# Counts stage of a graph network: rings of four for ScalarE's source lanes and columns, copies of sums three steps behind, one turning moved by a step

## The chip, the cores and the metric

The kernel runs on one core of a Trainium2 chip. The metric is the device time of one execution in microseconds (us). A core has five engines that work side by side and wait for each other through semaphores: PE (TensorE, matrix products), DVE (VectorE), ACT (ScalarE), POOL (GpSimd) and SP (SyncE, which here issues transfers). Each has a queue of its own that also runs its loops, register moves and branches. PSUM holds PE's results, SBUF everything else that is on the core.

## The reference

A graph of 3125 nodes with 96 features and 103125 directed edges goes through four layers, each with a residual sum and a layer norm:

```
edge_index = stack([src, dst])                                   # edges sorted by dst
x = layernorm(x + L0(x))   # 10 steps of h = segment_sum(h[src] * dinv[src] * dinv[dst], dst)
x = layernorm(x + L1(x))   # attention over the edges, 4 heads
x = layernorm(x + L2(x))   # message by edge type (8), 2 layers
x = layernorm(x + L3(x))   # 2 layers of two linear maps, summed over the edges
```

All layers use the same edges. So the kernel first turns the list of edges into a dense matrix of counts (how many edges go from node to node) and one of codes (which types they have), and the layers then multiply by it. The change is in the stage that makes these two matrices.

## The kernel before, in words

The nodes are padded to 3200 = 25 tiles of 128 (NT = 25). A tile of destinations has 8 windows of 16 (WPT = 8, DW = 16), 200 windows in all; a window has two halves of 8. The edges of a half window lie in some chunks of 128 edges (one in each partition); a group holds 3 chunks of each half (GRP = 3, PAIR = 6). With these inputs each window needs one group, so the inner loops over `groups` run once. For each window:

- POOL, `records`: reads from the table `tile_tab` in SBUF where the chunks of each half begin (two register loads, made by `load`, L358), waits until ACT has read the slot of the ring `rec` (RECS = 4 slots) that it will write, and copies the records of the chunks there with two small copies (L445).
- ACT, `chosen`: copies the source lane and the value of each record into `sel` (L627) and works out the column of each edge in the window into `col` (L629, with the window's offset `woff` as bias). Both have two slots, and L627 waits until DVE has made the codes of the window two before.
- DVE: makes one-hot matrices by comparing with `iota`: `srchot` (128 lanes of source, from `sel`, L474), `hot` (200 columns for each half, from `col`, L477), and `codehot` = `srchot` times the value (L480). Two slots each; L474 waits until PE has used those of two windows before.
- PE, `window`: opens a PSUM bank of `codes` and one of `counts` with two products of zeros (L550; RING = 3 banks each, so it waits first for ACT's copy of the window three before), multiplies `srchot` by `hot` for the six chunks (L555), then `codehot` by `hot` (L560), and closes with a product of zeros (L564).
- ACT, `window_out`: copies the window's counts into `ct`, the matrix in SBUF (L604), and its codes into `stage` (L606). This is done two windows behind: in the slot of window w, after `chosen`, come the sums of w - 2.
- PE, `turn_round`, and ACT, `row_out`: the tile before this one is transposed in four rounds of up to seven blocks (L572), each followed by a copy to `crow` that also sums up the degrees (L614). `turned_after` says after which of PE's windows a round comes; ACT takes the same round two windows later.
- SP: stores `stage` by quarters of a tile, 200 KB each, when both windows of the quarter are copied (L668); the tile's row of `crow`, 800 KB, behind quarter 2 of the tile after it (L677); and the tile's `ct`, 800 KB, behind its own quarter 3 (L672). SP works through these strictly in order.

The order of the work on each engine is thus written out by hand, and only semaphores tie the engines together. In a ring, the wait for a free slot is on a count kept in registers: `past` holds how many groups were done when earlier windows began. In `records`, `free` is the register `past[0]` itself, read after the moves have shifted it.

In the last tile ACT also takes the first of three square roots, in the slot of window 2 (`root(0)`, L649). After the last window DVE scales the features and splits them in two halves for the first layer (L496 to L503), and with that the stage ends. The first product of the next stage starts at 440.76 us.

Of the kernel before, what the change touches and what calls it, by code (L numbers as in the profile page):

```python
# [7 lines left out]
F16 = mybir.dt.float16  # L8
BF16 = mybir.dt.bfloat16
# [4 lines left out]
ACT = mybir.ActivationFunctionType  # L14
# [62 lines left out]
def gnn_kernel(nc, a, out):  # L77

    with ExitStack() as top:
# [283 lines left out]
        assert WC <= 256 and len(rounds) == NR and 2 * WC <= 512 and 2 * NR == WPT and WPS == 2 * WPT  # L363
        RING = 3

        turned_after = {1: 0, 3: 1, 4: 2, 5: 3}
        RECS = 4
        LAG = 5
        assert WPT % RECS == 0
        with ExitStack() as ph:  # L370
# [17 lines left out]
            s_sq, s_sqo = sem("l0_sqrt_in"), sem("l0_sqrt_out")  # L388
            rec = wqk[:, 114:114 + RECS * 2 * PAIR].rearrange("p (k g c) -> p k g c", k=RECS, c=2)
            rec_sv = wqk[:, 114:114 + RECS * 2 * PAIR].bitcast(F16).rearrange("p (k g c) -> p k g c", k=RECS, c=4)  # L390
            sel = wqk[:, 162:162 + 2 * PAIR].bitcast(F16).rearrange("p (k c g) -> p k c g", k=2, c=2)
            col = wqk[:, 174:174 + PAIR].bitcast(BF16).rearrange("p (k g) -> p k g", k=2)
            assert 114 + RECS * 2 * PAIR <= 162
            s_rec = sem("cnt_rec")
            assert NW * (NCHP // GRP) + 2 < 1 << 16
            s_col = sem("cnt_col")
# [23 lines left out]
            with nc.Block() as block:  # L420
# [34 lines left out]
                @block.vector  # L455
                def _(e):
                    c = Chain(e, s_prep)
                    e.memset(zero, 0.0).then_inc(s_zero, 1)
                    e.wait_ge(s_xt, 1)
                    e.tensor_reduce(xone[:], counts[0:1, 2, 0:P], AX_X, ALU.max).then_inc(s_xone, 1)  # L460
                    n, past, free = three(e, "dve")
                    every = lambda v, m: v.unsqueeze(1).to_broadcast([P, GRP, m, 2])
                    each = lambda v, m: v.rearrange("p (g c) -> p g c", c=2).unsqueeze(2).to_broadcast([P, GRP, m, 2])

                    def tile(t):
                        groups = groups_of(e, t)
                        for w in range(WPT):
                            k = w % 2
                            e.reg_mov(free, past)
                            e.reg_mov(past, n)  # L470
                            with e.Fori(0, groups):
                                e.wait_ge(s_used, e.snap(free) + 1)
                                e.wait_ge(s_sel, e.snap(n) + 1)
                                e.tensor_tensor(srchot[:, k, :, :, :], every(iota[:, 2, 0:P, :], P), each(sel[:, k, 0, :], P),  # L474
                                                ALU.is_equal).then_inc(s_one, 1)
                                e.wait_ge(s_col, e.snap(n) + 2)
                                e.tensor_tensor(hot[:, k, :, :, :], iota[:], each(col[:, k, :], WC),  # L477
                                                ALU.is_equal).then_inc(s_hot, 1)
                                e.wait_ge(s_one, e.snap(n) + 1)
                                e.tensor_tensor(codehot[:, k, :, :, :], srchot[:, k, :, :, :], each(sel[:, k, 1, :], P),  # L480
                                                ALU.mult).then_inc(s_code, 1)
                                e.reg_add(n, n, 1)
                                e.reg_mov(free, n)

                    def degrees(i):
                        ts = PARTS[i]
                        e.wait_ge(s_turn_out, NR * ts.stop + 2)
                        c(e.tensor_reduce(deg[:, ts], dacc[:, ts, :], AX_X, ALU.add))
                        c(e.tensor_scalar(dinv[:, ts], deg[:, ts], 1.0, None, ALU.max))
                        c(e.tensor_scalar(some[:, ts], deg[:, ts], 1.0, None, ALU.min))  # L490
                        e.reciprocal(rdeg[:, ts], dinv[:, ts]).then_inc(s_sq, 1)

                    def rows_scaled(i):
                        ts = PARTS[i]
                        e.wait_ge(s_sqo, i + 1)
                        c(e.tensor_tensor(dinv[:, ts], dinv[:, ts], some[:, ts], ALU.mult))  # L496
                        c(e.scalar_tensor_tensor(val[:, ts, :], x[:, ts, :], scale[:, 0:1],
                                                 dinv[:, ts].unsqueeze(2).to_broadcast([P, ts.stop - ts.start, D]), ALU.mult, ALU.mult))

                    def rows_split(i):  # L500
                        ts = PARTS[i]
                        c(e.tensor_copy(u[0][:, ts, 0, :], val[:, ts, :]))
                        c(e.tensor_tensor(u[0][:, ts, 1, :], val[:, ts, :], u[0][:, ts, 0, :], ALU.subtract))  # L503

                    with e.Fori(0, NT - 1) as t:
                        tile(t)
                    degrees(0)
                    tile(NT - 1)

                    power_of_two(c, e, power[:], xall[:], scale[:, 0:1])  # L510
                    c(e.tensor_scalar(scale[:, 1:2], power[:], 2.0 ** -14, None, ALU.mult))
                    rows_scaled(0)
                    e.wait_ge(s_used, e.snap(n) + 1)
                    rows_split(0)
                    degrees(1)
                    ROUND_UP = 12582912.0
                    c(e.tensor_scalar(gc[:, 1:2], gc[:, 1:2], ROUND_UP, -ROUND_UP, ALU.add, ALU.add))
                    c(e.tensor_tensor(gc[:, 1:2], gc[:, 1:2], gc[:, 0:1], ALU.subtract))
                    c(e.tensor_scalar(gc[:, 1:2], gc[:, 1:2], (GG - 1) / 2, 1.0 / GG, ALU.add, ALU.mult))
                    c(e.tensor_scalar(gc[:, 1:2], gc[:, 1:2], ROUND_UP, None, ALU.add))  # L520
                    last_tile = ident[0:NT, NT - 1:NT]
                    c(e.tensor_scalar(gc[:, 1:2], gc[:, 1:2], -ROUND_UP, last_tile, ALU.add, ALU.add))
                    c(e.tensor_scalar(gc[:, 1:2], gc[:, 1:2], float(SLOTS), last_tile, ALU.max, ALU.subtract))
                    c(e.tensor_copy(gi[:, 1:2], gc[:, 1:2]))
                    c(e.tensor_scalar(gc[:, 1:2], gc[:, 1:2], -float(GG), float(NCHG), ALU.mult, ALU.add))
                    c(e.tensor_scalar(gc[:, 0:1], gc[:, 0:1], gc[:, 1:2], None, ALU.min))
                    e.tensor_copy(gi[:, 0:1], gc[:, 0:1]).then_inc(s_gtab, 1)
                    rows_scaled(1)
                    rows_split(1)
                    degrees(2)  # L530
                    rows_scaled(2)
                    rows_split(2)
# [61 lines left out]
                def _(e):  # L594
# [20 lines left out]
                                     ACT.Copy, accum_out=dacc[:, bass.ds(t, 1), q]).then_inc(s_turn_out, 1)  # L615

                    e.sem_inc(s_code, 1)
                    n, past, free = three(e, "act")

                    def chosen(t, w, groups):  # L620

                        e.reg_mov(free, past)
                        e.reg_mov(past, n)
                        with e.Fori(0, groups):
                            e.wait_ge(s_rec, e.snap(n) + 1)
                            e.wait_ge(s_code, e.snap(free) + 1)
                            e.activation(sel[:, w % 2, :, :], rec_sv[:, w % RECS, :, 0:2].rearrange("p g c -> p c g"),  # L627
                                         ACT.Copy).then_inc(s_sel, 1)
                            e.activation(col[:, w % 2, :], rec[:, w % RECS, :, 1], ACT.Identity,  # L629
                                         bias=woff[:, bass.ds(t * WPT + w, 1)]).then_inc(s_col, 1)  # L630
                            e.reg_add(n, n, 1)
                            e.reg_mov(free, n)

                    def tile(t, first, second, last=False):
                        groups = groups_of(e, t)
                        for w in range(WPT):
                            chosen(t, w, groups)
                            if w >= 2:
                                window_out(t, w - 2, first)
                            elif not first:  # L640
                                window_out(t - 1, WPT - 2 + w, second)
                            if not first and w - 2 in turned_after:
                                row_out(t - 1, turned_after[w - 2], second)
                            if last and w == 2:
                                root(0)
# [7 lines left out]
                    with e.Fori(2, NT - 1) as t:  # L653
                        tile(t, False, False)
                    tile(NT - 1, False, False, True)
                    window_out(NT - 1, WPT - 2, False)
                    window_out(NT - 1, WPT - 1, False)
                    for q in range(NR):
                        row_out(NT - 1, q, False)
                        if q == 0:  # L660
# [1844 lines left out]
```

## Time and profile before

| | us |
|---|---|
| median of three runs | 2363.64 (2362.68 to 2366.68) |
| the profiled execution, its own time | 2366.91 |
| its span | 2365.2 |
| the counts stage in it, about | 47 to 440 |

Over the whole span the page has PE busy 91%, DVE 77%, ACT 49%, POOL 37%. These are means over stages with different limits. In the page's 40 slices of 59 us the counts stage is slices 1 to 7: there DVE is at 8 and 9 tenths, PE and ACT at 8, POOL at 4. The granted clock is at 9 tenths and more of the full 2.4 GHz in nearly all slices.

How to read the rows below: times are from the start of the span; a group of instructions is named by line, engine and operation, with what it writes and reads (`out<-in`). Several tensors are views of larger ones, and rows name those: `rec`, `sel` and `col` are parts of `wqk`, `srchot`, `crow` and `stage` parts of `flat`, `hot` and `codehot` parts of `onehots`. Idle time before an instruction is put down to what seems to have ended it. Register loads, moves and branches are in an engine's queue (POOLq, ACTq) and not in its busy time.

### The profile page before, as it was taken

Reading aid. Unit: us, or ns where it says so; the run is one execution under the profiler, and the core shown is the slowest. Engines: PE = TensorE matmul, PEld = TensorE weight load, DVE = VectorE, ACT = ScalarE, POOL = GpSimd, SP = SyncE. Lnnn points to the kernel's source line nnn. Section 1 sums busy time; section 2 is a strip of 40 time slices with the busy share of each in tenths; the row PEclk is TensorE's granted clock in tenths of the full one; section 3 lists DMA queues with packets and bytes.
Section 4 is the critical chain, followed back from the end, with each engine's and each line's share of the span. In section 5 each row is a group of like instructions: output and inputs, shape, how many; then the busy total and the mean of one; then the engine's idle time right before and its main releaser. Section 6 shows DMA issues by size and latency. Waiting matters only on the chain. (4 is left out here: it accounts for less than half of the span.)

```text
span 2365.2 us, 63175 instructions
## 1 busy us (share of the span) xinstructions
PE 2159.4 (91%) x22505; PEld 1795.4 (76%) x22506; DVE 1832.0 (77%) x2687; ACT 1162.6 (49%) x2789; POOL 879.4 (37%) x1062
## 2 busy tenths in 40 slices
PE   2888888799999999888999978999999999999897
PEld 2777777799999999622222225999996799999787
DVE  8899988765655566578999976988886788887446
ACT  1888888432332333388999966231322432230323
POOL 3444444000000000067888832555552455555000
PEclk8999999899999999989999979999998999999899
DMA  2344444200100000242222224223224322222800
GB/s 67 153 166 165 164 166 159 106 30 30 43 30 30 29 29 15 65 108 57 57 57 59 57 97 159 84 73 88 75 60 127 139 74 77 85 75 45 343 11 22
DMA packets 94785, 205.64 MB, mean 87 GB/s; under 512 B 21718, under 2 KB 61270, under 8 KB 94450
## 3 DMA queue, kind: packets, MB, share of 16 engines
q1 hardware_dynamic: 81458, 182.46, 22.3%
q0 software_dynamic: 13120, 20.18, 4.3%
q8 instruction: 159, 2.61, 0.5%
q14 instruction: 48, 0.39, 0.1%
HBM read 116.99 MB, written 84.76 MB: 85 GB/s over the span
## 5 line engine op out<-in xcount | busy, mean ns | idle before, releaser
L1873 PE MATMUL l_bank<-tab,mask 128*128 128x192 f16 x7600 | 636.3, 247 | 8.3 <-PEq L1704 3.5
L1873 PEld LDWEIGHTS l_bank<-tab,mask 128*128 128x128 f16 x7600 | 629.5, 98 | 10.8 <-issue 10.2
L1459 DVE TENSOR_SCALAR mask<-code 128x1600 int32<-128x1600 int32 x304 | 546.7, 1816 | 91.6 <-PE l_bank L1873 82.7
L1849 POOL DMA_INDIRECT ggot<-table_dram,gidx x408 | 386.2, 947 | 264.7 <-PE l_bank L1873 204.0
L1356 DVE TENSOR_TENSOR pr<-ex,count_copy 128x1568 f32<-128x1568 f32 x200 | 351.0, 1786 | 24.7 <-POOL ex L1255 12.8
L1346 ACT ACTIVATE ex<-score_pair,poss 128x784 f32<-128x784 f32 x400 | 344.0, 910 | 30.0 <-PE score_pair L1294 18.6
L1255 POOL TENSOR_SCALAR ex<-ex 128x1568 f32<-128x1568 f32 x200 | 298.5, 1493 | 78.2 <-ACT ex L1346 71.1
L891 PE MATMUL sums<-onehots,ct 128*128 128x192 f16 x3125 | 266.5, 250 | 11.6 <-issue 7.3
L891 PEld LDWEIGHTS sums<-onehots,ct 128*128 128x128 f16 x3125 | 263.9, 99 | 14.1 <-issue 7.9
L891 PE MATMUL sums<-u,ct 128*128 128x192 f16 x3125 | 259.1, 246 | 0.0
L891 PEld LDWEIGHTS sums<-u,ct 128*128 128x128 f16 x3125 | 258.0, 98 | 0.0
L445 POOL COPY wqk<-edges 128x6 f32 x400 | 162.4, 435 | 244.9 <-ACT wqk L629 133.2
L950 DVE TENSOR_REDUCE onehots<-sums 128x96 f32<-128x192 f32 x250 | 89.2, 357 | 178.7 <-PE sums L891 177.7
L1933 ACT ACTIVATE gidx<-rowidx 128x12 int32 x34 | 7.2, 211 | 426.2 <-PE l_bank L1881 396.1
L1294 PE MATMUL score_pair<-qa,ka 96*128 96x392 f16 x800 | 205.7, 340 | 3.6 <-ACT ex L1346 2.2
L1294 PEld LDWEIGHTS score_pair<-qa,ka 96*128 96x128 f16 x800 | 47.4, 98 | 184.9 <-ACT ex L1346 176.3
L1310 PE MATMUL att_acc<-pr,v 128*32 128x392 f32 x1600 | 176.6, 513 | 5.6 <-DVE pr L1356 5.6
L555 PE MATMUL counts<-onehots,flat 128*128 128x200 f16 x1200 | 145.9, 257 | 33.2 <-DVE onehots L477 31.2
L868 POOL PARTITION_ALL_REDUCE wtop<-wmax x1 | 0.4, 374 | 434.7 <-DVE wmax L981 434.7
L477 DVE TENSOR_TENSOR onehots<-iota,wqk 128x1200 f16<-128x1200 f16 x200 | 155.3, 776 | 0.0
L560 PE MATMUL codes<-onehots 128*128 128x200 f16 x1200 | 143.6, 255 | 0.0
L474 DVE TENSOR_TENSOR flat<-iota,wqk 128x768 f16<-128x768 f16 x200 | 111.7, 558 | 39.4 <-ACT wqk L627 32.6
(344 smaller groups left out, 2873.0 us busy)
## 6 DMA issues: line engine op xcount, KB each, us to landing
code<-code_dram SPq DMA_DIRECT2D x38, 800.0 KB
code_dram<-flat SPq DMA_DIRECT2D x100, 200.0 KB, 1.9
ct_dram<-ct SPq DMA_DIRECT2D x25, 800.0 KB, 3.5
c_dram<-flat SPq DMA_DIRECT2D x25, 800.0 KB, 3.4
ct_again<-ct_dram SPq DMA_DIRECT2D x25, 800.0 KB, 17.3
cring<-c_dram SPq DMA_DIRECT2D x200, 98.0 KB, 1.9
table_dram<-tab SPq DMA_DIRECT2D x50, 384.0 KB, 2.3
flat<-code_dram SPq DMA_DIRECT2D x19, 800.0 KB, 4.4
```

Source lines behind the costliest of these rows:

```text
L445: ins = e.tensor_copy(rec[:, w % RECS, h * GRP:(h + 1) * GRP, :], edge_rec[:, bass.ds(chunks[h], GRP), :])
L477: e.tensor_tensor(hot[:, k, :, :, :], iota[:], each(col[:, k, :], WC), ALU.is_equal).then_inc(s_hot, 1)
L555: e.matmul(counts[:, b, h * WC:(h + 1) * WC], chunk_of(srchot, k, j), chunk_of(hot, k, j), start=False, stop=False, skip_group_check=True)
L891: mm = e.matmul(sums[t % RS][:, 0:2 * D], ct[:, t, s, :], u[par][:, s, :, :].rearrange("p k d -> p (k d)"), start=(s == 0), stop=(s == NT ...
L1255: ins = e.tensor_scalar(ex[n % UR][:], ex[n % UR][:], EXP_HIGH, EXP_LOW, ALU.min, ALU.max)
L1294: mm = e.matmul(pair_ps[k][:, h, 0:QC], ka[0:D, k * HP2 + h, j * P:(j + 1) * P], qa[0:D, k * HP2 + h, b * QC:(b + 1) * QC], start=True, st ...
L1310: mm = e.matmul(acc[h * HW:(h + 1) * HW, b % 2, 0:QC], v[:, j, h, :], pr[n % UR][:, h, :], start=(j == 0), stop=(j == NT - 1), skip_group_ ...
L1346: e.activation(ex[n % UR][:, k * HP2:(k + 1) * HP2, :], pair_ps[k][:, :, 0:QC], ACT.Exp, scale=poss[:]).then_inc(s_ex[k], 1)
L1356: e.tensor_tensor(pr[n % UR][:], ex[n % UR][:], c_ps[n % 2][:, 0:QC].unsqueeze(1).to_broadcast([P, H, QC]), ALU.mult).then_inc(s_pr, 1)
L1459: e.tensor_scalar(turned.rearrange("p (s q d) -> p s q d", q=NQ, d=DQ // 2), words.rearrange("p (q s d) -> p s q d", q=NQ, d=DQ // 2), abs ...
L1849: e.indirect_dma_start(ggot[:, k, j, :], None, table_dram[:, :], bass.IndirectOffsetOnAxis(ap=gidx[:, k, j:j + 1], axis=0)).then_inc(s_ggo ...
L1873: mm = e.matmul(acc[k][:, 0:2 * D], mask[:, r % MR, s, :], tab[:, s, r, :], start=(r == 0 and s == 0), stop=(r == R - 1 and s == NT - 1))
```

## The change

`sel` and `col` get four slots (SELS) in place of two, and `col` moves from `wqk` to unused columns of `onehots`. DVE reads them by `w % SELS`. ACT keeps the same count of groups as POOL does, four windows back, so L627 of a window waits for the codes of the window four before. The sums are copied three windows behind (OUT_LAG = 3), so the last three windows of a tile are copied in the slots of windows 0, 1 and 2 of the next, and the last three of all after the loop. The first round of turning comes after window 2 of the next tile and not after window 1.

```diff
-        turned_after = {1: 0, 3: 1, 4: 2, 5: 3}
+        turned_after = {2: 0, 3: 1, 4: 2, 5: 3}
         RECS = 4
+        SELS = 4
+        OUT_LAG = 3
...
-            sel = wqk[:, 162:162 + 2 * PAIR].bitcast(F16).rearrange("p (k c g) -> p k c g", k=2, c=2)
-            col = wqk[:, 174:174 + PAIR].bitcast(BF16).rearrange("p (k g) -> p k g", k=2)
+            sel = wqk[:, 162:162 + SELS * PAIR].bitcast(F16).rearrange("p (k c g) -> p k c g", k=SELS, c=2)
+            col_at = 2 * PAIR * (P + WC) + 2 * NW
+            col = onehots[:, col_at:col_at + SELS * PAIR].bitcast(BF16).rearrange("p (k g) -> p k g", k=SELS)
...  DVE: sel[:, k, ...] and col[:, k, :] become sel[:, w % SELS, ...] and col[:, w % SELS, :]
-                    n, past, free = three(e, "act")
+                    n = e.alloc_register("cnt_act_done")
+                    past = [e.alloc_register(f"cnt_act_past{k}") for k in range(SELS)]
+                    for r in (n, *past):
+                        e.reg_mov(r, 0)
                     def chosen(t, w, groups):
-                        e.reg_mov(free, past)
-                        e.reg_mov(past, n)
+                        free = past[0]
+                        for k in range(SELS - 1):
+                            e.reg_mov(past[k], past[k + 1])
+                        e.reg_mov(past[SELS - 1], n)
                         with e.Fori(0, groups):
                             e.wait_ge(s_rec, e.snap(n) + 1)
                             e.wait_ge(s_code, e.snap(free) + 1)
...  ACT: sel[:, w % 2, ...] and col[:, w % 2, :] become sel[:, w % SELS, ...] and col[:, w % SELS, :]
                             chosen(t, w, groups)
-                            if w >= 2:
-                                window_out(t, w - 2, first)
+                            if w >= OUT_LAG:
+                                window_out(t, w - OUT_LAG, first)
                             elif not first:
-                                window_out(t - 1, WPT - 2 + w, second)
+                                window_out(t - 1, WPT - OUT_LAG + w, second)
...
-                    window_out(NT - 1, WPT - 2, False)
-                    window_out(NT - 1, WPT - 1, False)
+                    for w in range(WPT - OUT_LAG, WPT):
+                        window_out(NT - 1, w, False)
```

## Rows read from the trace of the kernel before

**Rows 1.** Windows view, 60 to 408 us: stretch, length, busy time of each engine, clock

```profile
60.00:408.00 348.00, 297.43 (x3357) 270.35 (x3355) 313.16 (x556) 293.14 (x923) 148.77 (x370) 0.99 0.41 161
```

**Rows 2.** Groups of DVE by line, 60 to 408 us: busy, mean | idle before

```profile
L474 DVE TENSOR_TENSOR flat<-iota,wqk 128x768 f16<-128x768 f16 x185 | 103.3, 558 | 34.8 <-ACT wqk L627 28.2 <-issue 4.0 <-PE codes L560 2.5
```

**Rows 3.** Timeline of POOL, tile 13: start, length, instruction, idle before

```profile
242.00 0.65 POOL L445 COPY wqk<-edges 128x6 f32 x2 [2.00 <-issue]
243.60 0.34 POOL L445 COPY wqk<-edges 128x6 f32 x2 [0.94 <-issue]
245.86 1.02 POOL L445 COPY wqk<-edges 128x6 f32 x2 [1.91 <-ACT wqk L629]
...
254.65 0.32 POOL L445 COPY wqk<-edges 128x6 f32 x2 [0.57 <-issue]
256.97 1.25 POOL L445 COPY wqk<-edges 128x6 f32 x2 [2.00 <-issue]
```

**Rows 4.** Timeline of POOL, last tile, its first and last pair

```profile
407.47 1.30 POOL L445 COPY wqk<-edges 128x6 f32 x2 [2.00 <-issue]
...
420.17 0.77 POOL L445 COPY wqk<-edges 128x6 f32 x2 [0.86 <-ACT wqk L629]
```

**Rows 5.** Timeline of ACT, tiles 12 and 13, and the last tile's table load

```profile
239.92 0.31 ACT L629 ACTIVATE wqk<-wqk,onehots 128x6 bf16<-128x6 f32 x1
...
247.00 0.21 ACT L627 ACTIVATE wqk<-wqk 128x12 f16<-128x12 f16 x1 [1.28 <-POOL wqk L445]
...
247.99 0.50 ACT L606 ACTIVATE flat<-codes 128x400 uint16<-128x400 f32 x1
...
254.69 0.22 ACT L627 ACTIVATE wqk<-wqk 128x12 f16<-128x12 f16 x1
...
256.64 0.25 ACT L627 ACTIVATE wqk<-wqk 128x12 f16<-128x12 f16 x1
...
415.07 1.28 ACT L649 ACT_TABLE_LOAD   x1
```

**Rows 6.** By line L358, three stretches: queue, ns min/median/max, first and last

```profile
L358 POOLq TENSOR_LOAD <-tile_tab x394: 273/278/889, 60.1 to 406.9; - x197
...
L358 POOLq TENSOR_LOAD <-tile_tab x2: 280/566/853, 244.3 to 244.7; - x2
...
L358 POOLq TENSOR_LOAD <-tile_tab x9: 273/275/312, 250.4 to 256.4; - x9
```

**Rows 7.** Timeline of SP, tile 13, issues; then DMA issues of the page: us to landing

```profile
243.78 0.33 SPq L677 DMA_DIRECT2D c_dram<-flat  x1
...
246.43 0.34 SPq L672 DMA_DIRECT2D ct_dram<-ct  x1
...
c_dram<-flat SPq DMA_DIRECT2D x25, 800.0 KB, 3.4
```

**Rows 8.** Timeline of DVE, tiles 13 and 24

```profile
243.95 0.56 DVE L474 TENSOR_TENSOR flat<-iota,wqk 128x768 f16<-128x768 f16 x1 [0.18 <-issue]
...
245.59 0.55 DVE L474 TENSOR_TENSOR flat<-iota,wqk 128x768 f16<-128x768 f16 x1
...
254.95 0.56 DVE L474 TENSOR_TENSOR flat<-iota,wqk 128x768 f16<-128x768 f16 x1 [0.45 <-ACT wqk L627]
...
414.16 0.56 DVE L474 TENSOR_TENSOR flat<-iota,wqk 128x768 f16<-128x768 f16 x1
...
416.73 0.56 DVE L474 TENSOR_TENSOR flat<-iota,wqk 128x768 f16<-128x768 f16 x1 [0.85 <-ACT wqk L627]
...
423.73 0.56 DVE L474 TENSOR_TENSOR flat<-iota,wqk 128x768 f16<-128x768 f16 x1
```

**Rows 9.** Timeline of PE, tile 24, windows 3 and 4

```profile
418.04 0.71 PE L555 MATMUL counts<-onehots,flat 128*128 128x200 f16 x6 [0.41 <-DVE onehots L477]
418.58 0.70 PE L560 MATMUL codes<-onehots 128*128 128x200 f16 x6
...
420.06 0.71 PE L555 MATMUL counts<-onehots,flat 128*128 128x200 f16 x6
```

More of the change, by code:

```diff
@@ L390, in gnn_kernel @@
             rec_sv = wqk[:, 114:114 + RECS * 2 * PAIR].bitcast(F16).rearrange("p (k g c) -> p k g c", k=RECS, c=4)
-            sel = wqk[:, 162:162 + 2 * PAIR].bitcast(F16).rearrange("p (k c g) -> p k c g", k=2, c=2)
-            col = wqk[:, 174:174 + PAIR].bitcast(BF16).rearrange("p (k g) -> p k g", k=2)
-            assert 114 + RECS * 2 * PAIR <= 162
+            sel = wqk[:, 162:162 + SELS * PAIR].bitcast(F16).rearrange("p (k c g) -> p k c g", k=SELS, c=2)
+            col_at = 2 * PAIR * (P + WC) + 2 * NW
+            col = onehots[:, col_at:col_at + SELS * PAIR].bitcast(BF16).rearrange("p (k g) -> p k g", k=SELS)
+            assert col_at + SELS * PAIR <= NT * 2 * D
+            assert 114 + RECS * 2 * PAIR <= 162 and 162 + SELS * PAIR <= 2 * D
             s_rec = sem("cnt_rec")
@@ L473, in tile @@
                                 e.wait_ge(s_sel, e.snap(n) + 1)
-                                e.tensor_tensor(srchot[:, k, :, :, :], every(iota[:, 2, 0:P, :], P), each(sel[:, k, 0, :], P),
+                                e.tensor_tensor(srchot[:, k, :, :, :], every(iota[:, 2, 0:P, :], P), each(sel[:, w % SELS, 0, :], P),
                                                 ALU.is_equal).then_inc(s_one, 1)
                                 e.wait_ge(s_col, e.snap(n) + 2)
-                                e.tensor_tensor(hot[:, k, :, :, :], iota[:], each(col[:, k, :], WC),
+                                e.tensor_tensor(hot[:, k, :, :, :], iota[:], each(col[:, w % SELS, :], WC),
                                                 ALU.is_equal).then_inc(s_hot, 1)
                                 e.wait_ge(s_one, e.snap(n) + 1)
-                                e.tensor_tensor(codehot[:, k, :, :, :], srchot[:, k, :, :, :], each(sel[:, k, 1, :], P),
+                                e.tensor_tensor(codehot[:, k, :, :, :], srchot[:, k, :, :, :], each(sel[:, w % SELS, 1, :], P),
                                                 ALU.mult).then_inc(s_code, 1)
@@ L626, in chosen @@
                             e.wait_ge(s_code, e.snap(free) + 1)
-                            e.activation(sel[:, w % 2, :, :], rec_sv[:, w % RECS, :, 0:2].rearrange("p g c -> p c g"),
+                            e.activation(sel[:, w % SELS, :, :], rec_sv[:, w % RECS, :, 0:2].rearrange("p g c -> p c g"),
                                          ACT.Copy).then_inc(s_sel, 1)
-                            e.activation(col[:, w % 2, :], rec[:, w % RECS, :, 1], ACT.Identity,
+                            e.activation(col[:, w % SELS, :], rec[:, w % RECS, :, 1], ACT.Identity,
                                          bias=woff[:, bass.ds(t * WPT + w, 1)]).then_inc(s_col, 1)
```

## The prediction

> **What bounds the kernel now.** The change touches one stage, some 47 to 440 us of the span, so I read that stage alone. First the busy times of its even part, 60 to 408 us: DVE is busy 313.16 of 348.00 us (90%), ACT 293.14, PE 297.43, POOL 148.77 (43%) [rows 1]. By busy time DVE bounds it, and its idle time lies before one instruction, L474: 34.8 us, of which 28.2 were ended by ACT's L627, the copy that fills `sel` [rows 2]. That is what a deeper ring would give back. So the question is who makes L627 late.
>
> Next, the order in time of POOL, which gathers the records that L627 copies. The pairs of copies (one pair for each window) start at 242.00, 243.60, 245.86 ... 254.65 and 256.97 [rows 3]. Windows 0 of tiles 13, 14 and 24 are the rows 242.00, 256.97 and 407.47 [rows 3, 4]: 14.97 us for one tile, 150.50 / 10 = 15.05 us for each of the next ten. That is the pace of the stage. The page puts POOL's idle time before 245.86 down to ACT L629. It can't be that one: the pair at 245.86 (tile 13, window 2) refills the slot of four windows earlier, whose L629 started at 239.92 and took 0.31 us [rows 5] (it is the fourth L629 before the one that follows L627 at 247.00, which copies this record). Its release was 5.6 us old. POOL waits for nobody here; it is slow by itself. What it does in the "idle" time stands under its queue: two register loads from `tile_tab` for each window (`records`, L439) and one for each tile, 394 in 60 to 408 us with a median of 278 ns [rows 6], and branches and register moves around them. The shortest step, 243.60 - 242.00 = 1.60 us, is that serial program with no disturbance; the step over a tile's end, with one load more, is 256.97 - 254.65 = 2.32. A tile undisturbed would be 7 x 1.60 + 2.32 = 13.5 us; 15.05 are observed, so 1.5 us a tile, some 36 us over 24 tiles, are disturbance.
>
> Third, what disturbs. A load of 853 ns lies in 243.3 to 246 us, and the nine of 249.6 to 257 take 273 to 312 ns [rows 6]. The two 800 KB stores of the tile are issued at 243.78 (L677) and 246.43 (L672) [rows 7]. So POOL's loads are slow while a big store runs, about 0.75 us for each store.
>
> The Trainium skill weighs against both readings. Its page "Perfetto Trace Analysis", section Identifying the Most-Contended Engine, takes the engine with the highest occupancy as the one to optimize; that would be DVE, and rival 1 is that case. The Trainium skill's "SBUF — State Buffer", section SBUF: two separate sides, says that DMA and engine accesses can't slow each other; for these register loads the trace disagrees (0.28 against 0.85 us beside a store), and by that rule the moved stores would be worth nothing.
>
> **The change part by part.** Sum against the profiled execution: 2366.91 us, span 2365.2; the runs have a median of 2363.64, 3.3 lower. I work out a difference and put it on the median.
>
> (a) `sel`/`col` rings of four (from two). ACT's L627 may then start when the codes of four windows ago are made, not two. ACT can't use this beyond one window: it needs the record, and L627 follows POOL's second copy at once wherever ACT is free. What ACT does gain is at most its own lateness: in tile 13 DVE waited 0.45 us before 254.95 [rows 8] while ACT was at a turned row. Where ACT is in time, the record isn't there: L627 at 247.00 starts 0.12 us after POOL's pair of 245.86 ends [rows 3, 5]. POOL's program has no wait that ACT would now end sooner, so the tile stays at 15.05 us. DVE's undisturbed step is 245.59 - 243.95 = 1.64 us [rows 8], 13.1 us a tile, still under POOL's pace. Saved in the even part: 0. Bounds: from below 0, from above the whole 28.2 us of rows 2.
>
> (b) Three register moves more per window on ACT. They run in ACT's queue while the activates before them are at work. 0; without that cover an estimated 0.1 us a window (a load that reads memory takes 0.28 [rows 6], moves must be far under it), which ACT's idle time takes: ACT is busy 84% [rows 1], 12.7 us of a tile's 15.05.
>
> (c) `OUT_LAG` 3: L604 and L606 copy a window's sums one slot later. PSUM has RING = 3 banks, and PE's window w waits for the copy of w - 3 (L548), which ACT now reaches only after `chosen` of w. L606 ends 247.99 + 0.50 - 247.00 = 1.49 us after L627 [rows 5], L474 starts 0.25 after L627, and PE's L555 starts 418.04 - 416.73 = 1.31 after L474 [rows 8, 9]: the copy is done 1.24 after L474. PE's two zeroing products stand between, so PE may start each window some 0.2 us later than now. That is a new wait on PE; queued behind it are the window's twelve products, and DVE waits for the last of them only two windows on: it ends 418.58 + 0.70 - 416.73 = 2.55 us after L474, two steps of DVE are 3.28, so 0.7 us are in hand. 0, bounds 0 and, were it all on the path, 0.2 x 200 = 40.
>
> (d) Turning of row 0 from after window 1 to after window 2, so windows 2, 3, 4, 5 all carry one on PE and slots 4, 5, 6, 7 on ACT (before: 1, 3, 4, 5 and 3, 5, 6, 7). A PE window with a turning takes 420.06 - 418.04 = 2.02 us [rows 9], four of them 8.1 (the last turns four blocks only), against 4 x 1.64 = 6.6 on DVE: PE falls 1.2 us behind in them. `hot` has two slots, so DVE of window 7 would wait for PE's window 5 by some 0.4 us, if DVE ran at its own pace. It doesn't, since two disturbed POOL steps fall there. Late in tile 24, it can. On ACT a slot with a row is 256.64 - 254.69 = 1.95 us [rows 5], four are 7.8 against POOL's 3 x 1.60 + 2.32 = 7.1: 0.7 us late at the next tile's window 0, made good in the slots that have no row.
>
> (e) Moved with (c) and (d): both stores, since SP waits for copies. L677 waits behind the quarter of windows 4 and 5, whose second copy moves a slot into the next tile, some 1.6 us later; L672 behind window 7, also 1.6 us. They stay as many and as large, and the time between them stays one to two slots. Each still meets POOL's pairs of loads: it lands 3.4 us after its issue [rows 7], of which I take the last 2 or so as moving data, and POOL comes round every 1.60. What a store costs depends on where the pair of loads falls: one load hit (0.57 us, from 0.85 - 0.28) at least, two (1.13) at most; before it was 0.75. Laying those 2 us over POOL's steps of tile 13, 1.6 us later than now, I estimate about 0.6 for L677 and 0.7 to 0.9 for L672, as before. 0, with bounds of (0.57 - 0.75) x 2 x 24 = -9 us and (1.13 - 0.75) x 2 x 24 = +18 us.
>
> (f) The end. In tile 24 ACT has the square root with its table load (1.28 us at 415.07 [rows 5]) after the copy of window 0's sums, in the new order after that of 23's window 7, whose sums are there sooner, so L474 of window 3 starts at 415.80 (414.16 + 1.64) and not at 416.73. Then DVE goes on at 1.64 up to window 5, and windows 6 and 7 wait for PE, which now turns in four windows in a row: window 7 at 423.1 and not 423.73 [rows 8]. POOL's last pair starts at 420.17 [rows 4] and isn't late. From there DVE's chain runs to the end of the stage, with no wait for another engine of over 0.3 us, and shifts with it: -0.6 us, bounds 0 and -2 (window 7 as soon as its record and DVE allow).
>
> Sum: 0 + 0 + 0 + 0 + 0 - 0.6: 2366.3 for the profiled execution, **2363.0 us** in the measure of the median.
>
> **Rivals.**
> 1. *DVE-bound.* If L627 is late by ACT's own fault, the rings give back the 28.2 us: 2335 us. For it: DVE's 90%. Against: POOL's starts sum to the tile's whole time with no release it waits for. 8%.
> 2. *Stores cheaper.* The stores land where a pair of loads is hit once: -9 us and the end's -1: 2354. For it: the phase is fixed by the kernel, the same in each tile, and will be another. 15%.
> 3. *Slower: stores dearer.* A store starts just as a pair of loads begins, both are hit, 24 times: up to +18, half of it if one of the two stores does so: 2372 to 2381. It decides once L677's data begin within 0.1 us before the first load of a pair. Nothing in POOL's program gives it back. 12%.
> 4. *Slower: four turnings in a row.* If ACT and PE late together hold up DVE by over 1.9 us a tile, the rest is lost each tile: 0.4 x 23 = +9: 2373. It needs ACT over 15.05 us a tile where it is busy 12.7, or PE's 0.2 of (c) to reach DVE. 4%.
>
> **How the numbers follow.** No change 61%, rival 1 8%, rival 2 15%, rival 3 12%, rival 4 4%. A measurement of this kernel tells 0.2%, 4.7 us, from no change. The likeliest's own range is 2359 to 2368. For 8 in 10 I take in most of rivals 2 and half of 3 and leave rival 1: 2353 to 2373. Faster 24%: rival 1, rival 2, and little of the main case's low side. Same 60%. Slower 16%: rivals 3 and 4.
>
> **What would show it.** Right: POOL's window 0 pairs still 15.05 us apart (14.7 to 15.4), its steps between stores 1.60, loads over 0.8 us only beside the stores; DVE's idle before L474 still over 25 us, now ended by L627 behind a POOL copy, less often behind L614. (c), (d): PE waits for ACT L606 or DVE for PE's L560 in windows 6 and 7. (e): issues of L677 and L672 1 to 2 us later against POOL. (f): L474 of the last window 0 to 2 us nearer to POOL's last pair. Wrong: POOL's steps under 1.60, or tiles under 14.5 us (POOL wasn't the pace), or over 15.6 (rival 3).

## The result, and the profile after

| | before | after |
|---|---|---|
| median of seven runs, us | 2363.64 (2361.87 to 2368.44) | 2372.59 (2368.60 to 2374.67) |
| the profiled execution | 2366.91 | 2374.67 |
| its span | 2365.2 | 2372.9 |

The ratio is 1.0032, with a 95% interval of 1.0021 to 1.0044: the changed kernel is slower by some 8 us. "No change" was forecast, at 2363.0 us; slower was given 16%.

The even part of the counts stage, in the view of rows 1, and DVE's group in the view of rows 2, both of the changed kernel:

```profile
60.00:408.00 348.00, 291.16 (x3261) 260.93 (x3259) 306.37 (x543) 288.00 (x898) 145.25 (x362) 0.95 0.41 157
```

```profile
L478 DVE TENSOR_TENSOR flat<-iota,wqk 128x768 f16<-128x768 f16 x181 | 101.0, 558 | 41.5 <-ACT wqk L636 23.7 <-PE codes L564 13.5 <-issue 4.0
```

Every engine does less in the same 348 us: four windows fewer (181 for 185). DVE's idle time rose from 34.8 to 41.5 us, and 13.5 of it are now ended by PE's codes, where it was 2.5. Read by itself that looks like the new waits of (c) and (d), and the waits view shows PE's too. Two rows of before, then the two that answer to them in the changed kernel, all for 60 to 408 us (who waits, for whom: us, times, longest):

```profile
PE codes L550 <- ACT flat L606: 14.6, 15, 1.2
...
DVE flat L474 <- PE codes L560: 2.5, 4, 0.9
```

```profile
PE codes L554 <- ACT flat L610: 51.4, 75, 2.3
...
DVE flat L478 <- PE codes L564: 13.5, 24, 1.5
```

But the stage's pace is still POOL's. Its timeline for tile 13 of the changed kernel, to be laid beside rows 3:

```profile
246.98 0.65 POOL L449 COPY wqk<-edges 128x6 f32 x2 [2.00 <-issue]
248.57 0.34 POOL L449 COPY wqk<-edges 128x6 f32 x2 [0.95 <-issue]
250.25 0.91 POOL L449 COPY wqk<-edges 128x6 f32 x2 [1.34 <-ACT onehots L638]
252.48 1.10 POOL L449 COPY wqk<-edges 128x6 f32 x2 [1.33 <-ACT onehots L638]
254.17 0.73 POOL L449 COPY wqk<-edges 128x6 f32 x2 [0.58 <-ACT onehots L638]
256.62 1.07 POOL L449 COPY wqk<-edges 128x6 f32 x2 [1.72 <-issue]
258.35 1.01 POOL L449 COPY wqk<-edges 128x6 f32 x2 [0.66 <-ACT onehots L638]
259.94 0.32 POOL L449 COPY wqk<-edges 128x6 f32 x2 [0.58 <-issue]
262.26 1.28 POOL L449 COPY wqk<-edges 128x6 f32 x2 [2.00 <-issue]
```

The tile takes 262.26 - 246.98 = 15.28 us, and the steps are 1.59, 1.68, 2.23, 1.69, 2.45, 1.73, 1.59, 2.32. The undisturbed 1.59 is still there. Two steps are long by 0.6 and 0.9 us, and three more by some 0.1. Of these three the first, the step behind window 1, is no disturbance: in every tile of both kernels it takes 1.67 us or more. SP's timeline of the same stretch (start, length, issue; L686 is the store of a turned row, L681 that of the tile's `ct`, L677 those by quarters) and POOL's register loads of the six steps from 248.57 on, each row one step (ns min/median/max):

```profile
250.38 0.33 SPq L686 DMA_DIRECT2D c_dram<-flat  x1
252.85 0.33 SPq L677 DMA_DIRECT2D code_dram<-flat  x1
253.39 0.34 SPq L681 DMA_DIRECT2D ct_dram<-ct  x1
256.59 5.14 SPq L677 DMA_DIRECT2D code_dram<-flat  x2
```

```profile
L358 POOLq TENSOR_LOAD <-tile_tab x2: 273/278/282, 249.2 to 249.6; - x2
...
L358 POOLq TENSOR_LOAD <-tile_tab x2: 311/597/883, 250.8 to 251.3; - x2
...
L358 POOLq TENSOR_LOAD <-tile_tab x2: 279/324/368, 253.1 to 253.5; - x2
...
L358 POOLq TENSOR_LOAD <-tile_tab x2: 547/708/869, 254.8 to 255.7; - x2
...
L358 POOLq TENSOR_LOAD <-tile_tab x2: 278/345/412, 257.2 to 257.7; - x2
...
L358 POOLq TENSOR_LOAD <-tile_tab x2: 273/277/281, 258.9 to 259.3; - x2
```

Loads of 0.88 and 0.87 us stand beside the two big stores, as before; the second pair is now hit twice (0.55 and 0.87). And two loads, 0.37 and 0.41 us, stand right behind the issues of *quarter* stores (252.85 and 256.59), which the prediction did not price.

The whole stage can be added up. POOL's queue between its first and its last pair holds register loads, other instructions and gaps. This table is worked out from all its records in each trace (us; "to DVE's last" is from POOL's last pair to the start of the last window's first one-hot, "rest" all that follows, "other" the other instructions of the queue and "gaps" the time between them; the copies run beside both and are not counted):

```
                  first pair  422 loads  other  gaps   first to last  to DVE's last  rest
before              47.76      152.3     123.3  96.8      372.40          3.56      1941.45
after               47.86      161.3     123.3  96.8      381.42          2.43      1941.22
```

Other instructions and gaps are the same to 0.1 us. A wait for another engine would be a longer gap, so the change makes POOL wait for nobody. Its loads take 9.0 us longer, the end gives back 1.1, and the start and the rest take -0.1: together 7.8, and the profiled executions are 2374.67 - 2366.91 = 7.76 us apart. The granted clock in the stretch fell from 0.99 to 0.95 of the full 2.4 GHz, with PE less busy; since POOL's time is accounted for by its loads, and "rest" is 0.2 us shorter, this is not where the time went.

### The profile page after: what moved, and what is told of

Its sections match the earlier page's. It is cut to its first block and busy times, and to the rows that moved or that the text cites. A ratio compares the mean times of both kernels' runs of the same rounds, so it can differ in the third digit from the quotient of the medians.

```text
span 2372.9 us, 63177 instructions
## 1 busy us (share of the span) xinstructions
PE 2161.2 (91%) x22505; PEld 1792.9 (76%) x22506; DVE 1829.7 (77%) x2687; ACT 1166.1 (49%) x2789; POOL 878.2 (37%) x1062
## 5 line engine op out<-in xcount | busy, mean ns | idle before, releaser
L1882 PEld LDWEIGHTS l_bank<-tab,mask 128*128 128x128 f16 x7600 | 629.4, 98 | 11.5 <-issue 10.7
L559 PE MATMUL counts<-onehots,flat 128*128 128x200 f16 x1200 | 151.4, 264 | 9.1 <-DVE onehots L481 3.8
L481 DVE TENSOR_TENSOR onehots<-iota,onehots 128x1200 f16<-128x1200 f16 x200 | 155.3, 776 | 0.0
```

The lines of the kernel that those rows point to most:

```text
L481: e.tensor_tensor(hot[:, k, :, :, :], iota[:], each(col[:, w % SELS, :], WC), ALU.is_equal).then_inc(s_hot, 1)
L559: e.matmul(counts[:, b, h * WC:(h + 1) * WC], chunk_of(srchot, k, j), chunk_of(hot, k, j), start=False, stop=False, skip_group_check=True)
L1882: mm = e.matmul(acc[k][:, 0:2 * D], mask[:, r % MR, s, :], tab[:, s, r, :], start=(r == 0 and s == 0), stop=(r == R - 1 and s == NT - 1))
```

## The experiments

All ratios are to the kernel before, run on the same chip beside it, with 95% intervals; 0.1% is 2.4 us. Its median was 2362.36 us beside the first group of runs (parts, one load), 2358.17 beside the second (deferred stores, packed table) and 2360.44 beside the third (parts on the packed table, quarters twice), so runs of different groups are compared by their ratios. GpSimd in the expectations is POOL.

**One part at a time.** Theory A: POOL's register loads, disturbed by stores whose phase against POOL moved. Theory D: the new waits of PE and DVE. (B: ACT's lateness is the pace. C: the rings' register moves cost. E, and later F: the four turnings in a row cost. G: the lag costs once POOL is off the path. In the expectation of `oneload_before` B stands for DVE and ACT as the pace, in that of `packed_before` for "POOL is not the pace".) The three parts were run alone.

```diff
# rings_only: the change, but
-        OUT_LAG = 3
+        OUT_LAG = 2
-        turned_after = {2: 0, 3: 1, 4: 2, 5: 3}
+        turned_after = {1: 0, 3: 1, 4: 2, 5: 3}
# lag_only: the kernel before, but
+        OUT_LAG = 3      # window_out(t, w - OUT_LAG), window_out(t - 1, WPT - OUT_LAG + w)
# turn_only: the kernel before, but
-        turned_after = {1: 0, 3: 1, 4: 2, 5: 3}
+        turned_after = {2: 0, 3: 1, 4: 2, 5: 3}
```

> Only the rings of four for sel and col; the sums are copied two steps behind and the first turning comes after window 1, as before. Theory A (GpSimd's serial program of register loads and copies paces the stage, and the change costs only by where the 800 KB stores meet its register loads): the stores stay where they were, so the time stays within 0.1% of the kernel before (2363.6 us) and GpSimd's 422 register loads between its first and last pair of copies still add up to about 152 us (161 in the changed kernel). Theory B (ACT's lateness is the pace, rings give it back): 20 to 28 us faster. Theory C (the rings themselves cost, by three more register moves on ACT): 3 to 9 us slower.

> Only the copies of the sums three steps behind (rings of two, first turning after window 1). Theory A: both 800 KB stores move by one to two steps and meet more of GpSimd's register loads, so most of the 9 us appear here: 2368 to 2373 us, loads 158 to 162 us in sum. Theory D (the cost is PE waiting for a PSUM bank that ACT now frees later, and DVE waiting for PE): also slower, but with the loads' sum at 152 us and idle time of DVE before L474 ended by PE's L560 over 8 us.

> Only the first turning moved from after window 1 to after window 2. Theory A: the stores are tied to the copies of the sums and not to this turning, and move by well under a step: within 0.15% of before, loads' sum 150 to 155 us. Theory E (four turnings in a row on PE and ACT are what costs): 4 to 9 us slower with the loads' sum at 152 us.

Measured: rings 2363.56 us, 1.0007 [0.9995, 1.0018]; lag 2371.73 us, 1.0043 [1.0027, 1.0059]; turning 2366.13 us, 1.0021 [1.0011, 1.0031], more than was expected of it. The rings can't be told from before, and the other two cost. The same sums over POOL's queue:

```
                  first pair  422 loads  other  gaps   first to last  to DVE's last  rest
rings_only          47.83      153.4     123.3  96.8      373.52          3.79      1937.52
turn_only           47.64      155.8     123.3  96.8      375.92          3.70      1934.95
lag_only            47.84      159.2     123.3  96.8      379.31          1.89      1938.46
```

Again only the loads differ: +1.1, +3.5 and +6.9 us, in the order of the times. For the lag Theory A's numbers held (2368 to 2373 us, loads 158 to 162). Of Theory D's two signs one is there, 22.7 us of DVE's idle time ended by PE, but the other, loads still at 152, is not, and POOL's gaps did not grow. With the ends (+0.2, +0.1, -1.7) this gives +1.3 us for the rings (1.0007 is 1.7), +3.6 for the turning (1.0021 is 5.0) and +5.2 for the lag, where 1.0043 is 10 with a low end of 6.4. The order holds, and the lag's size is not wholly found in its one profiled execution. The column "rest" shows why a single profile says so little of a few us: these stages are the same code and differ by up to 6.5 us. It is the loads of this stage, not a difference of two profiled totals, that carries the argument. The parts don't add up (1.1 + 6.9 + 3.5 = 11.5, together 9.0); a phase need not add up.

**Stores taken from the stage.** The stage's own 800 KB `ct` stores were moved to the next stage, in both kernels.

```diff
-                                if q == NQ - 1:
-                                    own(t - 1)
...  next stage, SP, behind each load of codes
+                            for j in range(2):
+                                own((kk - 1) * 2 * CPK + (2 * c + j))
```

> The kernel before, with the 800 KB store of each tile's counts (L672) taken out of the counts stage and issued in the next stage, two behind each code load. Theory A: about half of the 35.5 us that the stores cost GpSimd's register loads goes: a tile 14.3 us, loads' sum 133 to 140 us, 2343 to 2350 us. If something else paces the stage: no change.

> The changed kernel with the same store moved to the next stage. Theory A: it loses the own store's share of the 44.5 us, so 2346 to 2353 us, and is still 2 to 6 us slower than defer_before (the row's store and the quarters stay where the change puts them). Theory D (PE and ACT holding each other): 8 us or more slower than defer_before.

Measured: 2353.89 us, 0.9969 [0.9957, 0.9980], and 2356.14 us, 0.9988 [0.9977, 0.9999]. Both are slower than was expected of them (2343 to 2350 and 2346 to 2353). In the first the loads fell from 152.3 to 144.1 us, not to 133 to 140, and the last window of DVE starts 8.1 us earlier (415.65 against 423.73), against 7.3 by the ratio. The stores that remain hit more often than before (their share stands in the table of slow loads below). Of the changed kernel 145.6 us of loads are left, 1.5 more than of the one before: most of the 9.0 us went when this store went, though the phases of the others moved too. The 0.2% between the two is within the two intervals' reach.

**Loads taken from POOL.** If POOL's loads pace the stage, fewer must make it faster, and with POOL off the path Theory D's waits are seen alone. First, one load of two words instead of two loads of one; then both first chunks packed in one word of the table, one load, and two register operations.

```diff
# oneload_before
-                            for h in range(2):
-                                first = load(e, tile_tab[0:1, bass.ds(t, 1), 2 * w + h], 0, 2 * NCHP - GRP)
+                            _, firsts = nc.values_load_multi_w_load_instructions(
+                                tile_tab[0:1, bass.ds(t, 1), 2 * w:2 * w + 2]..., engines=[e.engine], ...)
+                            for first in firsts:
# packed_before, packed_after: table = second * 2048 + first, made once at the start
-                                first = load(e, tile_tab[0:1, bass.ds(t, 1), 2 * w + h], 0, 2 * NCHP - GRP)
+                            e.reg_load(both, tile_tab[0:1, bass.ds(t, 1), w:w + 1]...)
+                            e.reg_alu(firsts[0], both, 2047, ALU.bitwise_and)
+                            e.reg_alu(firsts[1], both, 11, ALU.logical_shift_right)
...
+                                first = e.snap(firsts[h])
```

> The kernel before, with GpSimd's two register loads of a window made one load of two registers (same values). Theory A: GpSimd's undisturbed step falls from 1.60 to 1.25 to 1.30 us, under DVE's 1.64, so GpSimd stops being the pace; a tile falls from 15.05 to 13.4 to 14.0 us and the kernel to 2325 to 2340 us; GpSimd begins to wait for ACT's L629. Theory B (DVE and ACT are the pace): no change within 0.2%.

> The kernel before, with the two first chunks of a window packed in one word of the table (first + 2048 * second, made by VectorE at setup), so GpSimd does one register load and two register operations in place of two loads. A load of two words in one instruction (oneload_before) had taken twice as long as one of one word and brought only 0.3%. Theory A (GpSimd's program is the pace): step undisturbed 1.35 us, half as many loads to disturb; a tile falls under 14.7 us, to where ACT and DVE hold each other (ACT copies the sums of w - 2 only when PE has them and so runs at most a window ahead): 2340 to 2352 us. Theory B (GpSimd not the pace): within 0.2% of oneload_before, 2355 us.

> The changed kernel with the same packed table. Theory A: with GpSimd off the path the rings and the lag of three do what they can: ACT runs ahead and DVE goes at its own 1.64 us a window, 13.4 to 14.0 us a tile, 2325 to 2340 us, faster than packed_before by 5 to 15 us: the sign of the change turns round. Theory D (the change costs by PE and ACT holding each other, whoever is the pace): slower than packed_before by 4 to 10 us.

Measured: 2355.42 us, 0.9972 [0.9963, 0.9982]; 2324.14 us, 0.9851 [0.9838, 0.9865]; 2333.85 us, 0.9893 [0.9878, 0.9908]. The first fell short of its expectation, the second went past it (2340 to 2352), and the third lies in its range. The first one's queue shows why: the loads of `oneload_before` in 60 to 400 us, and those of `packed_before` in 60 to 390, by line (ns min/median/max):

```profile
L438 POOLq TENSOR_LOAD <-tile_tab x185: 506/517/1681, 59.7 to 398.8; - x185
```

```profile
L443 POOLq TENSOR_LOAD <-tile_tab x191: 284/298/893, 60.9 to 379.8; - x191
```

A load of two words takes 517 ns, nearly twice the 278 of one [rows 6], and is hit for up to 1681. One load of one word is what saves. In `packed_before` the sum of loads is 101.3 us (223 of them) and the stage's windows are DVE's. Its windows view, its DVE timeline, and DVE's waits in 60 to 390 us:

```profile
60.00:390.00 330.00, 296.42 (x3509) 274.62 (x3508) 321.82 (x589) 300.67 (x966) 197.95 (x384) 0.99 0.46 177
```

```profile
224.96 0.56 DVE L482 TENSOR_TENSOR flat<-iota,wqk 128x768 f16<-128x768 f16 x1 [0.18 <-issue]
226.60 0.55 DVE L482 TENSOR_TENSOR flat<-iota,wqk 128x768 f16<-128x768 f16 x1
...
234.75 0.55 DVE L482 TENSOR_TENSOR flat<-iota,wqk 128x768 f16<-128x768 f16 x1
236.57 0.56 DVE L482 TENSOR_TENSOR flat<-iota,wqk 128x768 f16<-128x768 f16 x1
238.47 0.56 DVE L482 TENSOR_TENSOR flat<-iota,wqk 128x768 f16<-128x768 f16 x1 [0.18 <-issue]
```

```profile
DVE flat L482 <- issue: 4.3, 23, 0.3
...
DVE flat L482 <- ACT wqk L635: 1.7, 3, 1.0
```

DVE is busy 97.5%; a window takes 1.64 us undisturbed (226.60 - 224.96) and the tile 13.51. This is the DVE-bound stage of rival 1, reached by shortening POOL's program and not by the rings. With two of the variants below that can't be told from it, it is the fastest version run: 1.5% under the kernel before, 35 us.

The expectation that `packed_after` would be the faster of the two was wrong; it is slower by 0.4% (2333.85 against 2324.14). So here, with POOL off the path, a new wait of the change costs. The three parts were put on `packed_before` one by one, with the edits shown above.

> packed_before with only the rings of four. DVE's idle time before its first comparison is down to 6 us there, so the rings have nothing to give: within 0.1% of packed_before. If ACT's lead was still short: up to 3 us faster.

> packed_before with only the sums copied three steps behind. Theory F: within 0.15% of packed_before; ACT is no longer the one DVE waits for. Theory G: 6 to 10 us slower than packed_before, with PE waiting for L606's successor before its zeroing products.

> packed_before with only the first turning moved to after window 2. Theory F (once GpSimd is off the path, four turnings in a row on PE and four row copies in a row on ACT, 1.95 us each against DVE's 1.64, hold DVE up by 0.3 to 0.4 us a tile): 6 to 10 us slower than packed_before (2324.1), tiles 13.85 us against 13.5. Theory G (the lag of three is what costs there): as packed_before.

Measured: 2325.03 us, 0.9855 [0.9840, 0.9870]; 2325.28 us, 0.9855 [0.9840, 0.9870]; 2337.84 us, 0.9912 [0.9898, 0.9925]. By their ratios rings and lag can't be told from `packed_before` (their last window of DVE starts 0.6 and 1.6 us later than its), so Theory G falls. The turning costs 0.6% of the kernel, some 14 us (its last window starts at 401.72 and not at 387.67), which is more than the 6 to 10 expected. Of `packed_turn`, DVE's wait in 60 to 390 us, to be laid beside the 1.7 above:

```profile
DVE flat L482 <- ACT wqk L635: 10.9, 44, 1.0
```

ACT and then DVE of `packed_turn` in three of the four slots that carry a row:

```profile
239.86 0.22 ACT L635 ACTIVATE wqk<-wqk 128x12 f16<-128x12 f16 x1
...
242.01 0.23 ACT L635 ACTIVATE wqk<-wqk 128x12 f16<-128x12 f16 x1
...
243.97 0.24 ACT L635 ACTIVATE wqk<-wqk 128x12 f16<-128x12 f16 x1
```

```profile
240.38 0.55 DVE L482 TENSOR_TENSOR flat<-iota,wqk 128x768 f16<-128x768 f16 x1
242.27 0.56 DVE L482 TENSOR_TENSOR flat<-iota,wqk 128x768 f16<-128x768 f16 x1 [0.17 <-ACT wqk L635]
244.25 0.56 DVE L482 TENSOR_TENSOR flat<-iota,wqk 128x768 f16<-128x768 f16 x1 [0.26 <-ACT wqk L635]
246.15 0.56 DVE L482 TENSOR_TENSOR flat<-iota,wqk 128x768 f16<-128x768 f16 x1 [0.18 <-issue]
```

With a row in its slot ACT comes round every 1.96 to 2.15 us, and DVE's steps are 1.89, 1.98 and 1.90 and not 1.64. With the rows spread over the tile, as before, DVE waits 1.7 us for ACT and not 10.9.

**Do the quarter stores cost?** Each quarter of `stage` was stored twice, the second time into another tensor; nothing that is stored is different, and the two big stores stay as they are.

```diff
-                        e.dma_start(code_dram[...], stage[...]).then_inc(s_stored[q % 2], 16)
+                        for into in (code_dram, twice_dram):
+                            e.dma_start(into[...], stage[...]).then_inc(s_stored[q % 2], 16)
...  the waits on s_stored count twice as far
```

> The kernel before with each 200 KB store of a quarter's codes made twice, the second to another tensor in HBM that nobody reads. Nothing that the engines compute or wait for in order changes but the transfers. Theory A (GpSimd's register loads lose time to every store, the small ones too): the loads' sum rises from 152 by 5 to 15 us and the kernel's time by as much (2368 to 2378 against 2362), with GpSimd's steps beside the quarters 0.1 to 0.5 us longer. If only the 800 KB stores matter: within 0.15%.

Measured: 2377.95 us, 1.0078 [1.0064, 1.0092], or +18.4 us. A tile of POOL, 240 to 256 us, and its loads in 60 to 408 us:

```profile
239.99 0.95 POOL L446 COPY wqk<-edges 128x6 f32 x2 [1.84 <-issue]
242.10 0.98 POOL L446 COPY wqk<-edges 128x6 f32 x2 [1.16 <-ACT wqk L630]
244.30 0.91 POOL L446 COPY wqk<-edges 128x6 f32 x2 [1.23 <-ACT wqk L630]
...
255.80 0.95 POOL L446 COPY wqk<-edges 128x6 f32 x2 [1.84 <-issue]
```

The tile is 15.81 us. The same sums:

```
                  first pair  422 loads  other  gaps   first to last  to DVE's last  rest
twice_before        47.84      171.5     123.3  96.8      391.64          2.60      1932.35
```

Loads +19.2, end -1.0: +18.2 against 18.4 measured. That is more than the 5 to 15 us expected of the loads. Stores of 200 KB slow POOL's loads, and nothing else of POOL changes.

**Which stores slow which loads.** The traces also hold the packets of the transfers: 1600 bytes each in the 200 KB stores, 6400 in the 800 KB ones. So each load can be sorted by the packets that move while it runs. This table is worked out from those records: the time of the loads over 0.278 us each, in us, and in brackets how many take over 0.298.

```
                200 KB packets only   800 KB packets (or both kinds)   no packet
before                1.6 (11)                33.6 (79)                -0.3 (0)
rings_only            2.6 (12)                33.9 (76)                -0.4 (0)
turn_only             5.8 (31)                33.0 (75)                -0.4 (0)
lag_only              6.4 (41)                35.7 (75)                -0.3 (0)
after                 9.4 (53)                34.9 (75)                -0.3 (0)
defer_before          7.7 (34)                19.4 (48)                -0.4 (0)
defer_after           9.0 (49)                19.5 (46)                -0.3 (0)
twice_before         19.6 (77)                35.0 (76)                -0.3 (0)
```

A load beside which no store's packet moves never takes over 0.285 us in these kernels (202 to 271 such loads in each). What grows with the change is the column of the 200 KB packets, by 7.7 of the 9.0 us; the loads that meet an 800 KB store grew by 1.3. It is the same with the turning alone and with most of the lag alone. And in `defer_before`, where 14.2 us went with the `ct` stores, the quarters took 6.1 back.

## Why the prediction was wrong, point by point

*What bounds the stage*: right. POOL's serial program paces it: undisturbed steps of 1.59 us, other instructions and gaps equal to 0.1 us in all eight kernels that keep its program, and a program one load shorter gives 1.5%.

*(a) the rings* and *(b) the moves at 0*: right. `rings_only` can't be told from before; it is neutral on the packed kernel too.

*(c) the lag as a wait, at 0*: right as a wait. PE waits for ACT's copies 75 times for 51.4 us where it was 15 times and 14.6, DVE for PE's codes 13.5 us where it was 2.5, and none of it is on the path; `packed_lag`, where DVE is the bound, is neutral. The loads' time that the lag costs comes by (e).

*(d) four turnings in a row, at 0 behind POOL*: right as a wait. Its price without that cover, 0.4 us a tile or 9 us, was low: the part costs some 14 us on the packed kernel alone, and 10 with rings and lag beside it. And who is late was wrong there: PE was named as what DVE would wait for, and it is ACT, with its rows in four slots, 10.9 us against PE's 1.6. In the kernel with two loads a window the turning does cost, +3.5 us of loads, by (e).

*(e) the moved stores, at 0*: **this step failed.** It measured +9.0 us. That the cost lies in where stores meet POOL's loads was right, and so was the sign named as a risk in rival 3; the list of stores was not. The step priced the two 800 KB stores at 0, and they measured +1.3 (33.6 to 34.9 in the table of slow loads). It gave nothing to the four stores of 200 KB, which the change moves as well, and the loads that meet only their packets measured +7.7 (1.6 to 9.4; 53 slow loads and not 11). Of these 7.7, 4.1 lie at the two quarters of a tile that have no 800 KB store behind them (1.3 to 5.4) and so beside nothing else that was found to slow a load. The other 3.6 lie at the two that have one close behind. There a load that meets the quarter might else have met the big store, so how those 3.6 and the 1.3 are shared is not settled.

The shift of the big stores was sized well: counted from POOL's pair of window 0, medians over the tiles, the row store is issued at 3.48 us and not 1.75, and the `ct` store at 6.42 and not 4.43, 1.7 and 2.0 later where 1.6 was said. The two quarters that stand alone moved from 8.25 to 9.7 and from 12.1 to 14.4. The bound of +18 us held for the sum, but it had been worked out for the two big stores, so that is luck.

*(f) the end, at -0.6*: right in sign, -1.1 measured, but not by the waits that it names. Windows 6 and 7 were to wait for PE; they wait for ACT's copy, and PE's codes are waited for at window 4. After POOL's last pair at 429.28 (rows 4 have 420.17) DVE's last window starts at 431.72 (rows 8: 423.73):

```profile
429.28 0.47 POOL L449 COPY wqk<-edges 128x6 f32 x2 [0.81 <-issue]
```

```profile
426.23 0.56 DVE L478 TENSOR_TENSOR flat<-iota,wqk 128x768 f16<-128x768 f16 x1 [0.29 <-PE codes L564]
...
429.74 0.56 DVE L478 TENSOR_TENSOR flat<-iota,wqk 128x768 f16<-128x768 f16 x1 [0.15 <-ACT wqk L636]
431.72 0.56 DVE L478 TENSOR_TENSOR flat<-iota,wqk 128x768 f16<-128x768 f16 x1 [0.26 <-ACT wqk L636]
```

*The chances*: slower was given 16%. The bounds of (e), -9 to +18, with its estimate near the middle at 0, leave more on the slow side than rival 3's 12%; a term whose bounds are wider than the measurement's resolution can't carry a 60% chance of no change.

*Left open*: why, to the tenth of a us, the 200 KB stores and POOL's loads meet more often after the shift than before; why a load is slowed at all while a store's packets move; and 5 us of the lag's 10 that its one profile doesn't show. Whether rings of `stage` or another queue for the stores would take the disturbance away wasn't tried.

## What to carry to other kernels

An engine at 43% busy can be the pace of a stage, if its queue is full of register loads and branches: add up its queue's records between two of its own events before you name a bound. When a change moves transfers, list every transfer that moves, small ones too, and treat the sum of "where they fall" as a term with both bounds and no preferred middle. A cover such as POOL's slowness hides real costs: here four rows of ACT in a run held nobody up until POOL was made faster, and then cost 10 to 14 us. And where a trace keeps the packets of transfers, sort the slow instructions by the packets that move beside them: an issue time alone doesn't say when the data move.

## What the runs showed of the hardware that was not expected

- A register load of one word from SBUF on POOL takes 0.272 to 0.285 us while no store's packets move (0.280 to 0.299 in the packed kernels), up to 0.92 beside an 800 KB store and up to 0.58 beside one of 200 KB alone (0.62 where each is made twice); the second store of each quarter cost 19.2 us over 422 loads.
- A load of two words takes 0.517 us, nearly two loads' time, up to 1.68 beside a store. Packing two numbers in one word and splitting them with two register operations took the undisturbed step from 1.60 to 1.38 us (222.24 - 220.86 in POOL's timeline of `packed_before`).
